# A GRU with a mixture-of-experts layer behind it: the stretch ahead of the recurrence scanned in quarters and split in pairs, and all shared-expert units formed for 256 tokens

## The reference

```python
def cell(h, x):
    gi = x @ W_ih + b_ih
    gh = h @ W_hh + b_hh
    r = sigmoid(i_r + h_r); z = sigmoid(i_z + h_z)
    n = tanh(i_n + r * h_n)
    h_new = (1.0 - z) * n + z * h
...
combine = top-2 of softmax(x @ w_gate), normalised to sum 1
act = silu(gate) * up                       # 8 experts, 256 wide
routed = combine-weighted sum of act @ w_down
shared = silu_and_mul(x @ w_sh_gate_up) @ w_sh_down   # 1024 wide
y = x_in + routed + shared                  # 2048 tokens of 512
```

## Time and profile before

| | us |
|---|---|
| median of 3 runs | 1200.42 (1195.88 to 1204.8) |
| the profiled execution | 1195.19 |
| its span, first to last instruction | 1193.4 |
| start of the recurrence in the span | 49.28 |
| end of its last matmul | 1033.5 |
| end of the last matmul of all | 1179.0 |

### The profile page before, as it was taken

One profiled execution on the slowest core, in us unless ns is written; L12 is line 12 of the kernel. 1 busy time (PEld: TensorE's weight loads), 2 busy tenths in 40 slices (PEclk: granted clock), 3 DMA queues, 4 the chain that ended last, 5 costly groups with the idle time before them and its releaser, 6 DMA issues.

```text
span 1193.4 us, 35909 instructions
## 1 busy us (share of the span) xinstructions
PE 1036.9 (87%) x13452; PEld 623.1 (52%) x13452; DVE 850.0 (71%) x4089; ACT 573.3 (48%) x1877; POOL 206.2 (17%) x213
## 2 busy tenths in 40 slices
PE   2789888889999898999899989998998898889894
PEld 2556555556665454555455545554555454555452
DVE  5898999868889888677867787678787778721111
ACT  4755555655555543445344434443444444435442
POOL 0200011020110212111211121112120112233332
PEclk9999999999999999999999999999999999999897
DMA  8943455381864753623451234234342144488694
GB/s 307 402 147 97 144 180 186 107 205 56 294 237 173 197 193 73 230 75 61 125 178 29 55 101 166 56 55 174 129 126 55 28 143 134 121 296 278 181 288 56
DMA packets 68829, 183.13 MB, mean 153 GB/s; under 512 B 7737, under 2 KB 40288, under 8 KB 61344
## 3 DMA queue, kind: packets, MB, share of 16 engines
q1 hardware_dynamic: 45632, 107.74, 25.5%
q0 software_dynamic: 23024, 73.11, 23.1%
HBM read 137.01 MB, written 52.87 MB: 159 GB/s over the span
## 4 chain that ended last, share of the span: by engine, by line
PE 51%; DVE 27%; ACT 10%; issue 7%; DMA 3%; POOL 0%; POOLq 0%; SPq 0%; ACTq 0%; DVEq 0%
PE psG L715 17%; PE psG L721 14%; PE psU L778 6%; DVE arena L1046 5%; DVE arena L1044 5%; ACT arena L1429 4%; ACT arena L1425 4%; PE psS L824 3%; DVE arena L1054 3%; DVE arena L1069 3%; DVE arena L1065 3%; DVE arena L1056 3%; PE psD L790 3%; DVE arena L1048 2%; PE psO L845 2%
## 5 line engine op out<-in xcount | busy, mean ns | idle before, releaser
L715 PE MATMUL psG<-arena 128*32 128x384 f16 x4096 | 213.8, 329 | 76.1 <-DVE arena L1069 68.2
L1425 ACT ACTIVATE arena<-arena 128x32 f32<-128x32 f32 x256 | 58.6, 229 | 336.7 <-DVE arena L1048 335.3
L721 PE MATMUL psG<-arena 128*32 128x384 f16 x4096 | 211.9, 327 | 3.7 <-issue 3.7
L778 PE MATMUL psU<-arena 128*128 128x256 f16 (+1 forms) x1920 | 203.7, 253 | 0.2 <-DVE arena L940 0.2
L1044 DVE STREAM_TRANSPOSE arena<-psG 128x128 f32<-128x128 f32 x256 | 81.1, 317 | 144.8 <-PE psG L721 138.2
L778 PEld LDWEIGHTS psU<-arena 128*128 128x128 f16 x1920 | 157.7, 99 | 49.1 <-issue 13.6
L715 PEld LDWEIGHTS psG<-arena 128*32 128x32 f16 x4096 | 86.2, 96 | 175.0 <-DVE arena L1069 141.9
L1625 POOL DMA_INDIRECT y<-arena x55 | 87.6, 1593 | 393.4 <-DVE arena L1046 312.2
L721 PEld LDWEIGHTS psG<-arena 128*32 128x32 f16 x4096 | 109.9, 97 | 60.9 <-issue 4.4
L1046 DVE STREAM_TRANSPOSE arena<-psG 128x256 f32<-128x256 f32 x256 | 104.1, 407 | 0.0
L790 PE MATMUL psD<-arena 128*128 128x512 f16 x384 | 97.6, 382 | 4.9 <-DVE arena L1264 4.9
(11 more groups left out here) (166 smaller groups left out, 1557.7 us busy)
## 6 DMA issues: line engine op xcount, KB each, us to landing
arena<-expert_weights SPq DMA_DIRECT2D x39, 1536.0 KB, 8.6
arena<-wgu POOLq DMA_DIRECT2D x32, 512.0 KB, 5.5
expert_weights<-arena POOLq DMA_DIRECT2D x9, 1536.0 KB, 6.8
gi_scratch<-arena SPq DMA_DIRECT2D x84, 128.0 KB, 2.0
arena<-gi_scratch SPq DMA_DIRECT2D x14, 768.0 KB, 5.6
arena<-wd POOLq DMA_DIRECT2D x16, 512.0 KB, 5.7
arena<-x SPq DMA_DIRECT2D x8, 512.0 KB, 4.0
hidden_rows<-arena SPq DMA_DIRECT2D x16, 256.0 KB
```

Of the source, the lines that this page charges most:

```text
L715: e.matmul(psG[32 * j:32 * j + 32, 0:384], prev[:, c, 2:6].rearrange("p q n -> p (q n)"), whv[c][1][:, :, :, 32 * j:32 * j + 32], start=(c ...
L721: r = e.matmul(psG[32 * j:32 * j + 32, 0:384], prev[:, c, 0:4].rearrange("p q n -> p (q n)"), whv[c][0][:, :, :, 32 * j:32 * j + 32], star ...
L778: r = e.matmul(psU[u % 2][:, 256 * gu:256 * gu + width], half(W_GS + ex * 4 + c, pw)[:, o:o + 128], hh[:, 1 - ph, c, first:first + width], ...
L1425: e.activation(Ur, Ur, ACT.Tanh, scale=reg_tr).then_inc(th_r, 1)
```

## The change

Ahead of the recurrence:
- `W_ih` is loaded in four pieces instead of two, `W_hh` in five, each with its own semaphore, and time steps 32 to 63 of x get a buffer and a load of their own right behind them. The small operands (biases, identity, indices) are loaded after these.
- The scans are spread over both engines by pieces: VectorE takes pieces 0 and 2 and half of piece 3 of `W_ih` and four twelfths of `W_hh`; ScalarE the rest, three twelfths of `W_hh` ahead of its first halves.
- Only 2 of 6 pairs of `W_ih` (not 8 of 12 pieces) are split before the scan of `W_hh` is finished.
- The halves of both weight matrices are made 1024 columns at a time.
- ScalarE moves 8 of the first 12 gates out of PSUM, VectorE 4 (before 6 and 6). The spread of the second group of scales stands between gates 2 and 3.
- `recur(0)` waits for the low halves group by group. The halves and the sums of later x move behind the first steps; the start of the entries that use them moves by 1 to 3 steps.

The shared expert: every unit holds 256 tokens. The last pair, chunks 14 and 15, is due at step 256, all eight units, ahead of expert blocks with a due time above 256 (block 23 and later).

```diff
-NU = 8 * SINGLE // 2
-US = NU + 8 * (NCH - SINGLE)
+US = 8 * NBLK
...
     for u in range(US):
         n = u % 8
-        q = 2 * (u // 8) if u < NU else SINGLE + (u - NU) // 8
-        s = 32 * (u // 8 + 1) if u < NU else SUB * (q + 1)
-        due = s + 3.5 * n if u < NU else s + 2.0 * n if q < NCH - 2 else s + 24 + 2.0 * n if q < NCH - 1 else T + 56 + 5.0 * n
+        q = 2 * (u // 8)
+        s = 32 * (u // 8 + 1)
+        due = s + (3.5 * n if u < US - 8 else 0)
...
-            p.add("PE", ("s_unit", u, i), 0.37 if u < NU else 0.24, before, step=s, due=due)
+            p.add("PE", ("s_unit", u, i), 0.37, before, step=s, due=due)
...
-        last, due = (("s_down", 4 * (q - q % 2) + 7, q % 2), 32 * (q // 2 + 1) + 28) if q < SINGLE else (("s_down", NU + 8 * (q - SINGLE) + 7, 0), SUB * (q + 1) + 18)
+        last, due = ("s_down", 4 * (q - q % 2) + 7, q % 2), 32 * (q // 2 + 1) + 28
...
-            for q in range(2):
-                piece(wih, raw(W_IH + SHIFT + 6 * q, 6), 6 * q, 6, ld_ih[q])
-            for q in range(2):
-                piece(whh, raw(W_HH + SHIFT + 6 * q, 6), 6 * q, 6, ld_hh[q])
+            for q in range(4):
+                piece(wih, ih_raw(3 * q, 3), 3 * q, 3, ld_ih[q])
+            for q, (k, n) in enumerate(((0, 3), (3, 3), (6, 3), (9, 1), (10, 2))):
+                piece(whh, hh_raw(k, n), k, n, ld_hh[q])
+            load(x_src(1), x[:, 1024:2048], ld_x1)
...
-                e.wait_ge(hh_lo, 12)
                 e.wait_ge(h_start, 1)
...
                 for c in range(KC):
+                    if t == 0:
+                        e.wait_ge(hh_lo, (2, 3, 5, 6)[c])
...
             def low_hh(k):
-                low(raw(W_HH + SHIFT + k, 1), half(W_HH + k, 0), half(W_HH + k, 1), col(SHH), hh_hi, k + 1, hh_lo)
+                at = CH * (W_HH + 2 * k)
+                low(pair(hh_raw(2 * k, 2)), halves(at, 0), halves(at, 1), col(SHH), hh_hi, k + 1, hh_lo)
...
             x_low(0)
-            for k in range(8):
+            for k in range(2):
                 low_ih(k)
...
-            link(rowmax(mx[:, 44:45], raw(W_HH + SHIFT, 3)))
+            link(rowmax(mx[:, 38:39], hh_raw(6, 4)))
...
-            for k in range(8, 12):
+            for k in range(4, 6):
                 low_ih(k)
-            for k in range(12):
-                if k % 2:
-                    gates_out(k)
+            for k, ready in enumerate(((), (1, 4), (), (7,), (), (10,))):
+                for n in ready:
+                    gates_out(n)
                 low_hh(k)
...
             e.wait_ge(ld_ih[1], 16)
-            e.activation(ring(1, 0, 3), raw(W_IH + SHIFT + 9, 3), ACT.Abs, accum_out=mx[:, 42:43]).then_inc(ih_sum, 1)
+            sum_weights(ih_raw(3, 3), ring(1, 0, 3), 42, ih_sum)
+            e.wait_ge(ld_ih[3], 16)
+            sum_weights(ih_raw(9, 3)[:, 768:1536], ring(1, 3, 3)[:, 0:768], 45, ih_sum)
+            e.wait_ge(ld_hh[0], 16)
+            sum_weights(hh_raw(0, 3), ring(0, 0, 3), 36, hh_sum)
             e.wait_ge(scaled, 1)
             x_high(0)
-            for k in range(8):
+            for k in range(2):
                 high_ih(k)
-            for q in range(2):
-                e.wait_ge(ld_hh[q], 16)
-            e.wait_ge(ih_sum, 1)
-            e.activation(ring(1, 0, 9), raw(W_HH + SHIFT + 3, 9), ACT.Abs, accum_out=mx[:, 45:46]).then_inc(hh_sum, 1)
-            for k in range(3):
-                sum_x(k)
-            for k in range(8, 12):
+            e.wait_ge(ld_hh[1], 16)
+            sum_weights(hh_raw(3, 3), ring(0, 3, 3), 37, hh_sum)
+            e.wait_ge(ld_hh[4], 16)
+            sum_weights(hh_raw(10, 2), view(hb0 + 4096, 1024, F32), 39, hh_sum)
+            e.wait_ge(ld_x1, 16)
+            e.activation(view(hb0 + 8192, 1024, F32), x_src(1), ACT.Abs, accum_out=gcol[:, PX1:PX1 + 1]).then_inc(x1_sum, 1)
+            for k in range(2, 6):
                 high_ih(k)
```

More of the change, by code:

```diff
@@ L26 @@
 SHIFT = 2
+WSHIFT = 4
 ESHIFT = 4
@@ L178, in make_plan @@
         p.add("SP", ("x_load", b), 0, [("x_low", b - 1)] if b > 2 else [], due=3.0 * (b - 2))
-        p.add("ACT", ("x_high", b), 1.17, [("x_load", b)] + ([("gates", 12 * b - 13, 3)] if b > 2 else []), step=6, due=3.0 * (b - 2) + 1)
-        p.add("DVE", ("x_low", b), 1.25, [("x_high", b)], step=6, due=3.0 * (b - 2) + 1)
+        p.add("ACT", ("x_high", b), 1.17, [("x_load", b)] + ([("gates", 12 * b - 13, 3)] if b > 2 else []), step=8, due=3.0 * (b - 2) + 1)
+        p.add("DVE", ("x_low", b), 1.25, [("x_high", b)], step=8, due=3.0 * (b - 2) + 1)
     for n in range(12, 12 * NBLK):
@@ L186, in make_plan @@
             before = [("gates", n, c - 1)] if c else x + ([("gates_out", n - 2)] if n > 13 else [])
-            p.add("PE", ("gates", n, c), 0.37, before, due=due)
+            p.add("PE", ("gates", n, c), 0.37, before, step=1, due=due)
         p.add("ACT", ("gates_out", n), 0.57, [("gates", n, 3)] + ([("gates_store", n - NEV)] if n >= 12 + NEV else []), due=due)
@@ L197, in make_plan @@
         for i in range(4):
-            p.add("POOL", ("scan_load", j, i), 2.5, seen, step=2, due=2 + 4 * j)
+            p.add("POOL", ("scan_load", j, i), 2.5, seen, step=3, due=2 + 4 * j)
     for k in range(24):
@@ L201, in make_plan @@
     for k in range(12):
-        p.add("ACT", ("d_sum", k), 1.25, [("scan_load", k // 4 + 3, 3)] if k >= 4 else [], step=1, due=2 + 2 * k)
+        p.add("ACT", ("d_sum", k), 1.25, [("scan_load", k // 4 + 3, 3)] if k >= 4 else [], step=3, due=3 + 2 * k)
     for w in range(2):
@@ L259, in make_plan @@
                 before += [("sw_low", 11), ("scales", 0)] if q == 0 else []
-            p.add("PE", ("s_unit", u, i), 0.37 if u < NU else 0.24, before, step=s, due=due)
[L261 to L267, removed]
+            p.add("PE", ("s_unit", u, i), 0.37, before, step=s, due=due)
+        last = lambda u: ("s_down", u, 1)
+        p.add("ACT", ("s_gate", u), 0.4, [("s_unit", u, 7)] + ([("s_low", u - 3)] if u > 2 else []), due=due)
+        p.add("DVE", ("s_up", u), 0.45, [("s_gate", u)], due=due)
+        p.add("ACT", ("s_high", u), 0.44, [("s_up", u)] + ([last(u - 3)] if u > 2 else []), due=due)
+        p.add("DVE", ("s_low", u), 0.45, [("s_high", u)], due=due)
+        for tc in range(2):
             before = [("s_low", u)] + ([("s_down", u, 0)] if tc else [last(u - 1)] if u else [])
@@ L856, in _ @@
             spread_back(1, 2)
-            for n in range(4):
-                for c in range(KC):
-                    gates(n, c)
-            spread_cross(2, PHH, 4)
-            spread_back(2, 4)
-            for n in range(4, 12):
+            for n in range(12):
+                if n == 2:
+                    spread_cross(2, PHH, 4)
+                if n == 3:
+                    spread_back(2, 4)
                 for c in range(KC):
```

163 lines of the change are left out of this document (86 added, 77 removed).

## The result

The changed kernel takes 1210.94 us in the median of 5 runs (1209.93 to 1213.72), the kernel before 1202.18 (5 runs, 1195.88 to 1204.8): ratio 1.0076, interval 1.0046 to 1.0105. The forecast was 1193 with a range to 1207.

A forecast was written before the change was run, and what follows sets the result against it. Chains of dependent work were taken as the bound: waits in front, small instructions per recurrence step, block period in the tail. Front -5.7, recurrence 0, tail -2 gave 1187 profiled, plus 5.2 for the median: 1193 us, range 1178 to 1207.

The forecast's parts named there:

- The front: Ahead of the recurrence: earlier scans and scales and fewer halves shorten it by 5.7 us, bounds -3.0 to -7.5.
- Rival 4: Ahead of the recurrence: small operands or TensorE's slow first gates hold the second scale where it was; 1198 us, chance 0.06.
- The recurrence: The 255 steps stay 3.81 us apart, cost 0, bounds -5 and +5 for one stop that may vanish or come twice.
- `up(23)` comes 9 us later: Tail before block 23: 12.4 us more shared-unit work ahead of it, less 3.4 us of stops filled.
- The stop that I counted as filled: Tail before block 23: a 2.83 us wait for a transfer, counted with its low clock as 3.4 us filled.
- The expert stretch, -6: Tail from block 23 to the last down: without shared-unit fill 6 us less, bounds 0 to -25.
- The end, -5.1: End of the tail: s_add(15) moves away, so add(38) waits for add(37) alone and starts 5.1 us earlier.
- Rival 1: Expert blocks: period falls to 5.7 us and the hole goes, 11 us less than forecast, 1182; chance 0.22.
- Rival 2: Expert blocks: TensorE's idle time in each block lowers its clock, +33 us, 1226; chance 0.08.
- Rival 3: Expert blocks: s_add(14) and s_add(15) collide with the blocks' adds, making two holes, 1205 us; chance 0.14.
- a sign that the prediction is wrong: Expert blocks: the granted clock falling between blocks, where 1.00 was expected, would show the prediction wrong.
- The base: Whole kernel: the median lies 5.2 us above the profiled execution, turning 1187 into 1192.5, rounded to 1193.

The follow-up runs named there:

- x3_due: Changed kernel with the last pair's shared units due at step 312 + 5n in place of 256; ratio 0.9936 to the kernel before.
- x5_both: Changed kernel with the last pair due at step 312 + 5n and the adds of chunks 12 and 13 behind the last row gather; ratio 0.991.
- x7_pair12: Changed front with chunks 12 and 13 as a 256-token pair, chunks 14 and 15 alone as before; ratio 0.998 to the kernel before.
- x8_noadd: Changed kernel without the adds of blocks 23 to 37, their contribution to y left out; one run, expert blocks 97.5 us in place of 114.9.
- x9_ob3: Changed kernel with a third output buffer, so out(k) waits for add(k-3) in place of add(k-2); ratio 1.0057 to the kernel before.
- x10_both_ob3: Changed kernel with later due times for the last pair, adds of chunks 12 and 13 behind the last row gather, and a third output buffer; ratio 0.9924.
- x4_pool: Changed kernel with the adds of chunks 12 and 13 held back behind the last row gather on GpSimd; ratio 0.9975 to the kernel before.
- x11_front_ob3: Changed front with the old 128-token units, the add of chunk 13 behind the last row gather, and a third output buffer; ratio 0.9928.

## Why the prediction was wrong

*The front.* Right. Predicted were the cross near 26 (26.6), the second scale at 29.8 (29.76), a gain of 5.7 us (6.7 to the start of `recur(0)`). The stretch behind the scale was over-estimated by a little: the last low half ended at 43.35 and not at 44.5. The additional transfers, 6 and not 7 (two more of `W_ih`, three of `W_hh`, one of x), did not follow one another: the DMA share is 0.93 at 367 GB/s in the new first stage. The Trainium skill's fixed time of about 2 us for each transfer ("DMA: Bandwidth & Descriptors", anatomy of one DMA) is given there for DMAs issued from GpSimd, and these loads are issued from SP; the 12 us that it would make in a row, an estimate from that page, are not in the trace. Rival 4 falls. The front alone makes the kernel 0.8% faster.

*The recurrence.* Right in its sum, 984.3 against 984.2, and partly by luck: the 5.4 us stop at one step is not in the changed kernel's trace, and others of nearly the same sum are. The forecast had allowed that this stop may vanish; that it goes with the old units in every trace, it had not. What makes it was not tried.

*`up(23)` comes 9 us later.* This step failed; it came 23.4 us later. Its terms: the work in front was to be 12.4 us more. By the matmuls' distances it is 213 x 0.1095 + 60 x 0.2165 = 36.3 us in place of 15.1, so 21.2 more. Of this 3.9 are the last three pairs of downs, which I put behind `up(23)` (the downs were all given the same due time, ahead of block 23), and 5 are the rest of the pair of chunks 12 and 13, which I had finished before step 256. The stops were to be 3.4 less and are some 2 more. The stop that I counted as filled, 2.83 us before the first turn of rows, did shrink, to 0.88. The new one of 7.36 stands before the second turn, where the kernel before had none: that `s_add(12)` passes from before the tail to in front of `rows(8)` on GpSimd I did not look at, though the diff moves it by way of the pair. x3_due takes 15.6 us back by the place, x5_both 7.0 more by the queue, x7_pair12 brings the queue's stop back by the first pair alone.

*The expert stretch, -6.* This step failed too: the period was nearly right and the bound wrong. With no fill the planner put `up` part 3 beside `act_t` in every second block, just as worked out, and the period fell to 5.94 (5.73 by the 1.5 us saved in every second block). But in place of -6 the stretch measured +4.6, since the adds can't follow: x8_noadd, 97.5 us without them, x9_ob3 and x10_both_ob3. I had named the adds' chain with 5.1 us in quiet queues and 8.1 beside loads, and bounded the stretch with the 5.1. With the shorter distances between blocks, loads of weights come 3.6 to 5.3 us apart by turns, where in the kernel before they were 5.8 to 7.2 apart, and beside such a pair one add takes 11.7 and 12.2 us. That is what the three stops stand behind. The trace of before had a warning: the adds ahead of `rows(8)` are 10.9 us apart there (1046.88 and 1057.76). That the pairing of loads makes the late adds is read from the traces and was not tried by itself. The two misses, 14.4 us up to `up(23)` and 10.6 here, make the error of some 24 us.

*The end, -5.1.* Right, -5.7.

*The rivals.* Rival 1's period nearly came and its time didn't. Rival 2, a low clock in every block, falls: with TensorE idle in each block the clock is 0.99 in x8_noadd. It did fall behind two of the changed kernel's three stops, those of 4.1 and 8.9 us, which the text had named as a sign that the prediction is wrong. The oscillation by short idle gaps that the Trainium skill describes ("TensorE: Matmul & The Clock Gate", second failure mode) isn't seen over the stretch of x8_noadd. Rival 3, the adds, was the nearest with its 1205 and a chance of 0.14, but not by its mechanism: it had two stops made by `s_add(14)` and `s_add(15)`. These are issued ahead of `add(23)`, and the three stops stand behind single late adds of the blocks. It missed the add in front of `rows(8)`.

*The base.* I added the 5.2 us by which the profiled execution was below the median. That is right on the whole; more runs put the median 7 above it.

## What to carry to other kernels

When work is made into larger pieces, follow everything that a piece ends with: here its add to the output moved past other entries of an in-order queue, and one late gather behind it stopped TensorE for 7.4 us, with a granted clock of 0.71 in the 8.8 us after. Work that fills the holes of a latency chain costs little where it stands: with 15 us of it and no long stop the blocks took 102.2 us (x10_both_ob3), without it and without adds 97.5 (x8_noadd). Put in front of the chain it costs its full time. Where every operation of a kind waits for the landing of the one before, count them and multiply, under the load that is there, before calling the chain of matmuls the bound.

## What the runs showed of the hardware

An indirect add of 128 rows to y is 4.8 to 5.1 us from the next at the end of the kernel, where little else moves (before, x10_both_ob3). In the changed kernel it is 11.7 and 12.2 us where two loads of weights of 1.5 MB are issued 3.6 and 5.3 us apart around it (1108.27 and 1111.90 with the add at 1110.89, 1163.04 and 1168.30 with that at 1163.97). The granted clock fell from 2.4 GHz towards 1.2 behind a stop of 8.9 us in the changed kernel and came back only after some matmuls at half speed (stages of the changed kernel):

```profile
1177.70:1184.00 6.30, 6.29 (x25) 3.08 (x26) 0.91 (x2) 2.06 (x4) 2.59 (x2) 0.53 0.56 90
```

The length of the last stop alone doesn't tell whether the clock falls. Stops of 2.3 and 2.74 us (x4_pool), 3.3 (x11_front_ob3) and 3.5 us (at 1123.9 in the changed kernel) left the matmuls behind them at full speed. Behind stops of 2.71 us (x4_pool) and 2.62 (x7_pair12) six matmuls of 512 columns took 2.4 us in place of 1.46, and behind one of 0.69 us the last `down` of x8_noadd took 2.74, where behind the same two stops of 1.54 and 0.69 the changed kernel's took 1.47.
